# Attention outputs written straight to their places in SBUF, and a new order of work

## The reference

```python
s = einsum('bqhd,bkhd->bhqk', q, k) * scale
a = softmax(where(mask, s, min))
o = einsum('bhqk,bkhd->bqhd', a, v)        # then reshape to 256 features, @ W_o
```

## Time and profile before

| | |
|---|---|
| median of 3 runs | 3050.72 us (3048.83 to 3053.17) |
| the profiled execution | 3054.61 us, span 3052.8 us |
| TensorE | 2798.3 us busy, 92% |
| VectorE | 2007.6 us, 66% |
| ScalarE | 1401.3 us, 46% |
| POOL | 638.1 us, 21% |
| mean granted TensorE clock | 0.95 |
| bytes moved by DMA | 286.80 MB |

### The profile page before, as it was taken

The page is one execution under the profiler, slowest core; times in us unless marked ns, Lnnn a source line. Parts: engine busy times, 40 slices in busy tenths (PEclk is TensorE's granted clock), DMA queues, the critical chain, the costliest instruction groups (busy, mean ns, idle before and its releaser), DMA issues.

```text
span 3052.8 us, 47858 instructions
## 1 busy us (share of the span) xinstructions
PE 2798.3 (92%) x14941; PEld 1347.5 (44%) x14996; DVE 2007.6 (66%) x4848; ACT 1401.3 (46%) x2571; POOL 638.1 (21%) x967
## 2 busy tenths in 40 slices
PE   8899999999999998999988888889889998999899
PEld 5433334335536323334465566565542432332456
DVE  6778477643683865884365678676878584886631
ACT  3255635663443762664634233322215355577341
POOL 1010001121410110132134345324321000112320
PEclk9799989999999998999998999999998999899899
DMA  6323122323451322243176326421331041122521
GB/s 186 109 66 113 42 63 66 117 78 90 149 157 46 91 60 62 67 126 97 44 194 183 117 71 172 130 87 37 108 88 49 15 126 50 41 59 84 183 99 37
DMA packets 268156, 286.80 MB, mean 94 GB/s; under 512 B 70665, under 2 KB 207243, under 8 KB 267275
## 3 DMA queue, kind: packets, MB, share of 16 engines
q1 hardware_dynamic: 256651, 282.28, 31.4%
q0 software_dynamic: 11264, 1.46, 0.3%
HBM read 167.43 MB, written 114.72 MB: 92 GB/s over the span
## 4 chain that ended last, share of the span: by engine, by line
PE 71%; DVE 13%; issue 7%; DMA 4%; ACT 2%; POOL 2%; SPq 1%; DVEq 0%; ACTq 0%; POOLq 0%
PE ring_c L1404 11%; PE ring_b L1371 11%; PE ring_a L1327 11%; PE ring_a L1439 7%; PE ring_b L1427 7%; PE ring_a L1416 4%; PE ring_b L1370 3%; PE ring_b L1284 3%; DVE row_max L1689 2%; ACT probs L1512 2%; PE ring_b L1398 2%; PE ring_a L1427 1%; PE ring_a L1299 1%; DMA q_ring<-neg_max_parts 1%; PE ring_b L1249 1%
## 5 line engine op out<-in xcount | busy, mean ns | idle before, releaser
L1512 ACT ACTIVATE probs<-ring_b 128x512 f32<-128x512 f32 (+1 forms) x1728 | 906.4, 602 | 518.0 <-PE ring_b L1371 453.9
L1689 DVE TENSOR_REDUCE row_max<-ring_a 128x1 f32<-128x1024 f32 x512 | 603.6, 1219 | 153.5 <-PE ring_a L1327 148.8
L1371 PE MATMUL ring_b<-q_ring,k_ring 100*128 100x512 bf16 x1536 | 521.8, 388 | 30.0 <-ACT probs L1512 13.4
L1327 PE MATMUL ring_a<-k_ring,q_ring 96*128 96x512 bf16 x1536 | 491.5, 414 | 37.9 <-DVE row_max L1689 17.9
L1404 PE MATMUL ring_c<-probs,v_and_ones 128*17 128x512 f32 x3072 | 402.3, 601 | 4.7 <-ACT probs L1512 4.6
L1795 POOL CAST neg_max_parts<-neg_max 16x128 bf16<-16x128 f32 x112 | 33.0, 295 | 1633.3 <-ACT neg_max L1506 1299.4
L1686 DVE CUSTOM_DVE_ANT_0 w_mlp<-ring_a,w_mlp 128x1024 bf16<-128x1024 f32 x256 | 302.7, 1222 | 60.5 <-PE ring_a L1327 58.7
L1327 PEld LDWEIGHTS ring_a<-k_ring,q_ring 96*128 96x128 bf16 x1536 | 131.0, 100 | 375.7 <-issue 295.5
L1371 PEld LDWEIGHTS ring_b<-q_ring,k_ring 100*128 100x128 bf16 x1536 | 144.4, 99 | 328.9 <-issue 228.1
L1733 DVE TENSOR_TENSOR x_tok<-x_tok,ring_a 128x512 f32<-128x512 f32 x96 | 66.0, 687 | 336.8 <-PE ring_a L1439 207.1
L1427 PE MATMUL ring_b<-h_feat,w_mlp 128*128 128x512 f32 x512 | 229.2, 594 | 3.9 <-ACT h_feat L1483 1.7
(11 more groups left out here) (145 smaller groups left out, 3496.6 us busy)
## 6 DMA issues: line engine op xcount, KB each, us to landing
q_ring<-scr_q SPq DMA_DIRECT2D x128, 384.0 KB, 4.3
scr_q<-split SPq DMA_DIRECT2D x64, 384.0 KB, 2.6
k_ring<-scr_k SPq DMA_DIRECT2D x64, 384.0 KB, 5.1
scr_q<-split SPq DMA_DIRECT2D x64, 256.0 KB, 3.0
scr_out<-out_stage SPq DMA_DIRECT2D x128, 128.0 KB, 2.6
scr_out<-out_stage SPq DMA_DIRECT2D x64, 256.0 KB, 2.2
h_feat<-scr_out SPq DMA_DIRECT2D x56, 256.0 KB
reciprocals<-scr_recip SPq DMA_DIRECT2D x56, 256.0 KB
```

The source lines that it names most:

```text
L1327: last = mm(ps[:, half * BLOCK:(half + 1) * BLOCK], q[0:PARTS, h, t * P:(t + 1) * P], k_view(g)[0:PARTS, h, half * BLOCK:(half + 1) * BLOC ...
L1371: last = mm(ps[:, :], k_view(g)[0:ROWS, h, s.kt * P:(s.kt + 1) * P], q[0:ROWS, h, q0:q0 + BLOCK], start=not g.masked, stop=True)
L1512: f(PT[0:n, s.pt, :], ps[0:n, :], ACT.Exp, **kw).then_inc(b_evac, 1)
L1689: v.tensor_reduce(NM[:, s.nm, s.u:s.u + 1], ps, AX.X, ALU.max).then_inc(a_evac, 1)
```

## The change

The DRAM copy `O_SCR` and the step "dense" are gone. The step "put" now waits for the last projection and V of this attention (they read `HT`), and for the last user of the denominator buffer, and then copies from the staging tile within SBUF: per tile of 32 rows the 16 output rows to their partitions of `HT`, in one or two pieces of tokens (`pieces`), then per token block the denominator rows to `DENC`. A full group issues 6 DMAs, a window group 8, a cross group 5. All raise the semaphore of the staging buffer. `DENC` is taken before the first product of a half of the heads. "recip" waits on the staging semaphores. "recip_put" stores one DMA per block. The constants of the order have new values, and the plan's costs of the changed steps too.

```diff
-        self.od_in = {}
+        self.recip_out = [0] * DENC_BUFS
...
-RANK = {... init=[9, 9, 9, 9], mod=[7, 0, 0, 0], prep=[3, 3, 7, 4], out=[1, 3, 7, 0], ctx=[0, 7, 3, 0], load=[3, 2, 5, 0], cross_f=[4, 4, 0, 8], cross_s=[4, 6, 8, 0], mlp=[2, 2, 2, 2], self_f=[0, 6, 6, 7], self_pv=[7, 6, 9, 9], self_s=[7, 4, 4, 1], tk=[1, 1, 1, 1], tk_s=[5, 5, 6, 5], win_f=[9, 9, 9, 9], win_s=[0, 0, 2, 0] ...}
-REACH = dict(PE=0.05, ACT=0.25, DVE=1.2, POOL=5, SP=0.1)
-YIELD = dict(ACT=2, DVE=-0.5, POOL=2, PE=0)
+RANK = {... init=[4, 5, 5, 5], mod=[6, 0, 0, 0], prep=[3, 3, 4, 4], out=[0, 3, 0, 2], ctx=[0, 8, 8, 8], load=[1, 1, 1, 5], cross_f=[0, 6, 4, 7], cross_s=[2, 4, 4, 0], mlp=[0, 0, 0, 0], self_f=[2, 5, 6, 7], self_pv=[7, 6, 7, 7], self_s=[8, 4, 4, 5], tk=[0, 0, 0, 0], tk_s=[5, 5, 7, 5], win_f=[1, 1, 1, 1], win_s=[4, 4, 3, 4] ...}
+REACH = dict(PE=0.05, ACT=0.05, DVE=0.05, POOL=1.2, SP=0.05)
+YIELD = dict(ACT=1, DVE=-0.5, POOL=-0.5, PE=1)
 DELAY = [7.5, 200.0]
-SECOND = dict(init=4, mod=-4, prep=-2, out=-6, ctx=-2, load=-6, cross_f=0, cross_s=4, mlp=-4, self_f=-1, self_pv=2, self_s=-1, tk=0, tk_s=-1, win_f=2, win_s=6)
-LATER = [-2.5, 8.5, -4.5, -4.5]
+SECOND = dict(init=-1, mod=-6, prep=-2, out=-4, ctx=-6, load=-6, cross_f=-6, cross_s=-4, mlp=0, self_f=1, self_pv=2, self_s=-4, tk=-1, tk_s=0, win_f=-1, win_s=-1)
+LATER = [-4.5, 4.5, -2.5, -4.5]
...
                 if kt == 0:
+                    if n % per == 0:
+                        c, dc_last, c_uses = yield ("get", "DENC")
+                        den = Step(c=c, c_last=dc_last, uses=c_uses)
...
-            w = yield do("put", [("SP", 0.9)], after=[s], lat=3.2, of=s, g=unit.g, ost=ost, uses=o_uses)
+            pieces = {"full": 6, "window": 8, "cross": 5}[kind]
+            w = yield do("put", [("SP", 0.47 * pieces)], after=[s, last_proj, den.c_last], lat=2.6, ...)
...
-        d = yield do("dense", [("SP", 0.6 + 0.6 * len(blks))], after=puts + [c_last, last_proj, v], lat=4.8, ...)
-        s = yield do("recip", [("DVE", 0.2 + 0.12 * len(blks))], after=[d], counts=["recip_n"], of=d)
-        put = yield do("recip_put", [("SP", 0.6)], after=[s], lat=3.2, of=d, rec=s)
+        s = yield do("recip", [("DVE", 0.2 + 0.12 * len(blks))], after=puts, counts=["recip_n"], of=d)
+        put = yield do("recip_put", [("SP", 0.55 * len(blks))], after=[s], lat=3.0, of=d, rec=s)
...
+        def pieces(st, blk):
+            lo = blk * BLOCK
+            if st.akind != "window":
+                return [(lo, lo + BLOCK, 0)]
+            if blk == 0:
+                return [(SHIFT, SHIFT + BLOCK, 0)]
+            return [(lo + SHIFT, TOKENS, 0), (0, SHIFT, BLOCK - SHIFT)]
...
-                    h0 = g.heads[0]
-                    n = len(g.heads) * VROWS
-                    for k, blk in enumerate(g.blks):
-                        sp.dma_start(O_SCR[g.b, h0:h0 + len(g.heads), :, blk * BLOCK:(blk + 1) * BLOCK].rearrange("h r t -> (h r) t"),
-                                     OST[k * n:(k + 1) * n, s.ost, :]).then_inc(ost_out[s.ost], 16)
-                elif s.kind == "dense":
-                    ...
                     product_done(s.last_proj)
                     if s.v is not None:
                         product_done(s.v)
+                    if s.den.c_last is not None:
+                        sp.wait_ge(norm_done, s.den.c_last.norm_n + 1)
+                    o, landed = OST[:, s.ost, :], ost_out[s.ost]
+                    for tile in range(4):
+                        head = g.heads[tile] if g.cross else g.heads[tile % 2]
+                        blk = g.blks[0] if g.cross else tile // 2
+                        hh, to, at = head // 8, head % 8 * HEAD, tile * VROWS
+                        for lo, hi, frm in pieces(s.st, blk):
+                            sp.dma_start(HT[to:to + HEAD, hh, g.b, lo:hi], o[at:at + HEAD, frm:frm + hi - lo]).then_inc(landed, 16)
+                    to = g.heads[0] % 8 * HEAD
+                    n = len(g.heads)
+                    for k in range(len(g.blks)):
+                        at = k * n * VROWS + HEAD
+                        sp.dma_start(DENC[to:to + n * HEAD, s.den.c, k * 32:k * 32 + 32], o[at:at + (n - 1) * VROWS + 1:VROWS, :])\
+                            .then_inc(landed, 16)
```

More of the change, by code:

```diff
@@ L237, in do @@
     return Step(kind=kind, ph=ph, after=list(after), counts=list(counts), **kw)
[L240 to L242 removed]
+RANK = {k: tuple(r) for k, r in dict(init=[4, 5, 5, 5], mod=[6, 0, 0, 0], prep=[3, 3, 4, 4], out=[0, 3, 0, 2], ctx=[0, 8, 8, 8], load=[1, 1, 1, 5], cross_f=[0, 6, 4, 7], cross_s=[2, 4, 4, 0], mlp=[0, 0, 0, 0], self_f=[2, 5, 6, 7], self_pv=[7, 6, 7, 7], self_s=[8, 4, 4, 5], tk=[0, 0, 0, 0], tk_s=[5, 5, 7, 5], win_f=[1, 1, 1, 1], win_s=[4, 4, 3, 4]).items()}
+REACH = dict(PE=0.05, ACT=0.05, DVE=0.05, POOL=1.2, SP=0.05)
+YIELD = dict(ACT=1, DVE=-0.5, POOL=-0.5, PE=1)
 DELAY = [7.5, 200.0]
[L244 to L245 removed]
+SECOND = dict(init=-1, mod=-6, prep=-2, out=-4, ctx=-6, load=-6, cross_f=-6, cross_s=-4, mlp=0, self_f=1, self_pv=2, self_s=-4, tk=-1, tk_s=0, win_f=-1, win_s=-1)
+LATER = [-4.5, 4.5, -2.5, -4.5]
 def rank_of(kind, l, b, blk):
@@ L631, in products @@
         kind = st.akind
+        per = st.groups // KF
+        last_proj = yield ("flag", key + ("projected",))
         for n in range(st.groups):
@@ L656, in products @@
                 p.give("PC", 0, s)
-            w = yield do("put", [("SP", 0.9)], after=[s], lat=3.2, of=s, g=unit.g, ost=ost, uses=o_uses)
+            pieces = {"full": 6, "window": 8, "cross": 5}[kind]
+            w = yield do("put", [("SP", 0.47 * pieces)], after=[s, last_proj, den.c_last], lat=2.6, of=s, g=unit.g, ost=ost,
+                         uses=o_uses, st=st, den=den, last_proj=last_proj, v=None if st.cross else v)
             p.give("OST", ost, w)
             w.before = p.ost_out[ost]
-            p.ost_out[ost] += 16 if st.cross else 32
+            p.ost_out[ost] += 16 * pieces
             w.need = p.ost_out[ost]
@@ L669, in dense @@
     def dense(st, key, hh, blks):
[L670 to L674, removed]
-        puts = [st.puts[n] for n in range(hh * st.groups // KF, (hh + 1) * st.groups // KF)]
[L676 to L681, removed]
-        s = yield do("recip", [("DVE", 0.2 + 0.12 * len(blks))], after=[d], counts=["recip_n"], of=d)
-        put = yield do("recip_put", [("SP", 0.6)], after=[s], lat=3.2, of=d, rec=s)
+        puts = [st.puts[n] for n in range(hh * st.groups // KF, (hh + 1) * st.groups // KF)]
+        den = puts[0].den
+        d = Step(st=st, hh=hh, blks=blks, c=den.c, uses=den.uses, puts=puts, b=st.b, l=st.l)
+        s = yield do("recip", [("DVE", 0.2 + 0.12 * len(blks))], after=puts, counts=["recip_n"], of=d)
+        put = yield do("recip_put", [("SP", 0.55 * len(blks))], after=[s], lat=3.0, of=d, rec=s)
+        p.recip_out[d.c] += 16 * len(blks)
+        put.need = p.recip_out[d.c]
         for blk in blks:
@@ L688, in dense @@
             r.need = p.rb_in[e]
-            s = yield do("normalise", [("DVE", 0.62)], after=[r, d], counts=["norm_n"], of=d, got=r, blk=blk)
+            s = yield do("normalise", [("DVE", 0.62)], after=[r], counts=["norm_n"], of=d, got=r, blk=blk)
             p.give("DEN", e, s)
             p.raise_flag(key + ("normed", hh, blk), s)
-        p.give("DENC", c, s)
+        p.give("DENC", den.c, s)
     def topk_units(st, key):
@@ L953, in blocks_kernel @@
         ost_out = [sem(f"out_stage_written_{i}") for i in range(OST_BUFS)]
-        den_in = [sem(f"denominators_in_{i}") for i in range(DENC_BUFS)]
         recip_done = sem("reciprocals_done")
@@ L957, in blocks_kernel @@
         rb_in = [sem(f"reciprocals_in_{i}") for i in range(DEN_BUFS)]
-        od_in = {(b, hh, k): sem(f"dense_in_{b}_{hh}_{k}") for b in range(BATCH) for hh in range(KF) for k in range(BLOCKS)}
         norm_done = sem("out_normalised")
@@ L1185, in _ @@
                     sp.wait_ge(recip_done, s.rec.recip_n + 1)
-                    t0, span = d.blks[0] * BLOCK, len(d.blks) * BLOCK
-                    sp.dma_start(R_SCR[d.c, :, t0:t0 + span].rearrange("h (c t) -> h c t", c=HEAD), DENC[:, d.c, 0:span // HEAD])\
-                        .then_inc(recip_out[d.c], 16)
+                    for k, blk in enumerate(d.blks):
+                        sp.dma_start(R_SCR[d.c, :, blk * BLOCK:(blk + 1) * BLOCK].rearrange("h (c t) -> h c t", c=HEAD),
+                                     DENC[:, d.c, k * 32:k * 32 + 32]).then_inc(recip_out[d.c], 16)
                 elif s.kind == "recip_get":
                     d = s.of
-                    sp.wait_ge(recip_out[d.c], 16 * d.uses)
+                    sp.wait_ge(recip_out[d.c], s.put.need)
                     if s.e_last is not None:
@@ L1719, in _ @@
                     n = len(d.blks) * BLOCK // HEAD
-                    dve.wait_ge(den_in[d.c], 16 * d.uses)
+                    for ost in range(OST_BUFS):
+                        need = [w.need for w in d.puts if w.ost == ost]
+                        if need:
```

(1 more changed line is left out.)

5 lines of the change are left out of this document (removed).

## The result

The forecast was 3027 us and faster. The changed kernel takes 3077.39 us (median of 4 runs, 3073.94 to 3083.41) against 3049.77 for before in the same comparison: ratio 1.0088, 95% interval 1.0065 to 1.011. It is slower by 28 us and within the stated range (2982 to 3090), on the side that had 0.26.

What follows compares the result with a forecast made beforehand. TensorE was taken as the bound, busy 2798.3 of 3052.8 us. Latency -3, traffic -4, SP's queue +3 and order -20 gave -24 us on 3054.6, or 3030.6; 3.9 lower for timed runs: 3027 us, range 2982 to 3090.

Steps and rivals of the forecast that it cites:

- The latency of one chain: Staging store to reciprocal: a bare cross chain goes from 4.96 to 4.6 us; about -3 us over the kernel.
- the 5.9 us that I worked out beside it: Cross chain's store to reciprocal if the denominator copy takes 3.9 us to land: 1 us worse than now.
- SP in front of others: 212 us more issues on SP stand ahead of weight, scratch and q loads: +3 us (0 to +20).
- Traffic: 33 of 286.8 MB of DMA bytes go, shrinking TensorE's waits that end in a DMA: -4 us (0 to -12).
- The order: Replanned instruction order places projections sooner and fills less, mainly between 1500 and 2300 us: -20 us (-60 to +45).
- Rival 3: SP's issues set the rate of short groups; ScalarE waits for staging buffers, TensorE stops: +35, about 3086 us; chance 0.15.
- Rival 4: Three denominator buffers, held longer, make the next half's products wait up to 11.5 us: +46, about 3097 us; chance 0.11.
- Rival 1: Whole DRAM round trip goes and the plan uses it, VectorE's and TensorE's waits mostly vanish: about 2980 us; chance 0.17.

Runs made afterwards that it cites:

- den_first: Changed kernel, same order, with denominator rows issued ahead of the output pieces on a semaphore of their own: 3075.29 us, ratio 1.0075.
- pad_before: Kernel before, same order and path, plus 544 extra 16 x 16 copies of a constant issued by SP, which nothing waits for: 3078.06 us, ratio 1.0084.
- pad_half: Kernel before with 272 extra 16 x 16 copies of a constant issued by SP: 3062.22 us, ratio 1.0037.
- no_pieces: Changed kernel, same order, without the 544 copies of outputs, only the 192 denominator copies kept: 3029.25 us, ratio 0.993.
- path_only: Kernel before's order on every compute engine, with direct copies from the staging tile and eight small denominator places: 3088.18 us, ratio 1.0119.
- tiny_pieces: Changed kernel, same order and 736 issues, but each output piece carries 16 tokens of its 512: 3078.46 us, ratio 1.0081.
- searched_before: Kernel before with its own path and its order's constants searched anew: 3034.37 us, ratio 0.9944.
- pool_searched: Changed kernel with all copies from the staging tile issued by POOL instead of SP, constants searched for that: 3055.84 us, ratio 1.0017.

## Why the prediction was wrong

- *"The latency of one chain", 4.6 us after against 4.96.* The term was about right: a bare chain takes 4.41 us (2943.37 to 2947.78). An issue took 0.61 there where I took 0.5 (I went by the store of the same tile; the one-row copy at 0.55 was nearer), and the denominators landed in 1.9 us where I took 2.6. The two errors nearly cancel, and that was luck. My reading of the earlier trace rows was wrong, though: the chain of 4.96 us is not bare, VectorE was busy with other tokens up to the reciprocal. In three of the five places where VectorE did wait for such a load, issue to use took 2.0 to 2.3 us; the last chain's load went out at 2957.75, so the path itself needed an estimated 2957.75 + 2.0 (to 2.3) - 2955.50 = 4.3 to 4.6 us. The change won or lost next to nothing here. The rows of the kernel before, the last chain's load first:

```profile
2957.75 0.60 SPq L1177 DMA_DIRECT2D denominators<-scr_out  x1
2959.17 1.38 DVE L1595 TENSOR_SCALAR x_norm<-x_tok,mean_var,rstd 128x256 f32<-128x256 f32 x4
...
2917.64 0.60 SPq L1177 DMA_DIRECT2D denominators<-scr_out  x1
2919.65 0.35 DVE L1721 RECIPROCAL denominators<-denominators 128x32 f32<-128x32 f32 x1 [1.99 <-DMA denominators<-scr_out]
```

  The Trainium skill (DMA: Bandwidth & Descriptors, "Bandwidth") calls transfers under 64 KB dominated by their descriptors; the 5.9 us that I worked out beside it did not come, for pieces of 32 KB landed in 2.0 us (den_first).
- *"SP in front of others", +3 us (0 to +20).* This is the step that failed. I had the count (736) and the amount (212, in fact 277 us) and priced it at nearly nothing because the queue "mostly waits". Its price by itself is 26 us for 544 issues (pad_before), 11 for half (pad_half), and up to 48 for the 544 copies in the changed order (no_pieces against the result, landing included). With pad_before's median issue of 0.42 us that is 26 / 229 = 0.11 us of time per us of issue; 277 us then give an estimated 31 of path_only's 36. The forecast missed by 51 us: 28 of it are this term (3 against 31), the order's are some 10, the gains of the latency and of the traffic that did not come are 7, and 5 us of path_only are explained by no term. Why a queue that waits most of the time is not free time, I can only argue: it waits for the very operands whose consumers are next, and what becomes ready together goes out one after the other.
- *"Traffic", -4 us.* The bytes went (33 MB) and no time with them: tiny_pieces carries hardly any output bytes and takes as long as the changed kernel.
- *"The order", -20 us.* At best its sign was right against its own path, from 1.0119 (path_only) to 1.0088, 10 us that are not clear of noise; with the path of before it costs 45 us. Idle plus filling between 1500 and 2300 us fell from 266 to 259 us, not by 20, and over the whole span it rose from 475 to 485. searched_before shows that a fresh search can give 17 us, on the path of before.
- *Rival 3* named the cause, SP's issue time, and the wrong victim. ScalarE's waits for the staging tile came to 3.2 us, not tens, in 2 places:

```profile
  DMA denominators<-out_stage: 3.2, 2
```

  Its time, 3086, was near, its mechanism wasn't there; that was luck too, and by its own rows a cross put of 2.5 us against a pace of 1.43 lacks 1.07 us and not the 0.6 it used. The price was paid by other steps of SP's list.
- *Rival 4* did not happen: SP's wait for a denominator place in the changed kernel is the row below, 2.8 us in one place, and path_only had eight places and was no faster.

```profile
SPq L1171 <- DVE h_feat L1731: 2.8, 1, 2.8
```

- *Rival 1* needed issues of 0.315 us, the shortest single store of the earlier trace rows; the shortest piece of the changed kernel took 0.507.

What stays open: which DMAs behind the extra issues carry the loss, and whether SP's time or the copy's place in the queue is the price. All waits of TensorE that a DMA ended came to 46.6 us before and 45.7 in pad_before, no rise at all, while VectorE's wait for reciprocals rose by 21 us. TensorE's waits for VectorE rose from 112.9 to 121.2 us, those without a releaser that the profile shows from 11.3 to 19.5, and its busy time by 8.5 with the same matmuls, at a mean granted clock of 0.946 against 0.950. The loss is spread over many small gaps and I did not isolate one of them.

## What to carry to other kernels

Count a change of path in issues of its in-order queue first, and in bytes and latency second: here 544 more issues cost 26 us with nobody waiting for them, while 33 MB less, and denominators issued four issues sooner, gave nothing that could be measured. Before a chain is called bare, look whether the engine at its end was idle. An order searched for one set of prices belongs to that path; moving the path and keeping the order or its constants, or the reverse, cost 1.2% to 4.6%, so compare a change of path only with a search of equal effort on the old one. Relief of a queue paid where the queue that took the work had room (layers 0 and 1), and was lost where the latter feeds TensorE too.

## What the runs showed of the hardware

- A DMA of 16 partitions takes SP 0.589 us to issue by the median, with 2 KB or with 64 bytes per partition (tiny_pieces, the same 0.589), as a load of 128 partitions does (0.585): the bytes do not set the time. A copy of 16 rows of 64 bytes from a constant tile to DRAM took 0.421 by the median (pad_before).
- The pieces landed in 2.0 us by the median whether SP issued them (den_first) or POOL (pool_searched). POOL took 0.487 us to issue one.
- A copy of denominator rows, two or four source partitions, was in use 1.84 to 2.10 us after its issue by SP, in ten of VectorE's 17 waits for one. Issued by POOL the page gives 2.3 us.
